# Attention's first chunk: gates read between the query taps, scores and turned keys moved forward into another pair of banks, and unread products in two holes

## What is computed

```python
k, v, q = (causal_dwconv(x @ W.T, cw, cb) for ...)        # four taps each
alpha, eta, theta = ...                                   # three rates per token, from x
for c0 in range(0, S, 128):                               # 8 chunks of 128 tokens
    g = grad of sum((silu(k W1') W2' - v)**2) in W1, W2   # at the chunk's first state
    g = 0.1 * g, clipped to norm 1
    per token: Sm = eta * Sm - theta * g;  Wm = (1 - alpha) * Wm + Sm
    h = silu(q . W1_t);  out_t = h . W2_t                 # with each token's own state
out = rmsnorm(out @ Wo.T) * norm_g * (x @ gW.T + gb)
x = x + out
```

## Time and profile before

| | |
|---|---|
| median of three runs | 743.92 us (741.38 to 745.2) |
| the profiled execution | 744.58 us |
| its span | 742.7 us |
| PE busy | 653.0 us, 88% |
| DVE busy | 567.4 us, 76% |
| ACT busy | 430.5 us, 58% |
| POOL busy | 247.9 us, 33% |
| attention, from its first to its last matmul | about 195 to 575 us of the span |
| mean granted TensorE clock | 0.958 of full |

### The profile page before, as it was taken

How to read it: one execution, slowest core, us unless ns; L and a number is a source line. 1 busy time by engine, 2 the same in 40 slices (tenths; PEclk the granted TensorE clock), 3 DMA queues, 4 the chain that set the end, 5 groups by cost and what they waited for, 6 DMA issues and landing times. The chain is left out here.

```text
span 742.7 us, 15297 instructions
## 1 busy us (share of the span) xinstructions
PE 653.0 (88%) x5555; PEld 573.8 (77%) x5555; DVE 567.4 (76%) x1379; ACT 430.5 (58%) x1094; POOL 247.9 (33%) x199
## 2 busy tenths in 40 slices
PE   4539999999697899999999999999988379999995
PEld 2238889898576788989888898988866158999985
DVE  0867888773388989898898988888676878887851
ACT  1416585562355767687786777776543445667450
POOL 0033453123311536162452516243241061751302
PEclk9759999999899999999999999999999589999998
DMA  9959727160332105325141432604123624652401
GB/s 337 413 207 349 268 96 263 48 209 23 128 115 86 59 29 162 97 82 177 57 136 66 132 126 59 200 2 139 62 66 105 227 75 164 237 193 113 142 8 36
DMA packets 63586, 101.98 MB, mean 137 GB/s; under 512 B 8200, under 2 KB 50336, under 8 KB 63392
## 3 DMA queue, kind: packets, MB, share of 16 engines
q1 hardware_dynamic: 51536, 83.01, 32.5%
q0 software_dynamic: 3840, 10.49, 4.3%
q10 hardware_dynamic: 8144, 7.61, 3.3%
HBM read 87.31 MB, written 22.16 MB: 147 GB/s over the span
## 5 line engine op out<-in xcount | busy, mean ns | idle before, releaser
L726 PE MATMUL ps<-moe_normedT_high,weights_high_up 128*128 128x320 f32 x252 | 80.5, 320 | 1.0 <-DVE moe_hidden_low L544 0.8
L727 PE MATMUL ps<-moe_normedT_low,weights_high_up 128*128 128x320 f32 x252 | 77.9, 309 | 0.0
L728 PE MATMUL ps<-moe_normedT_high,weights_low_up 128*128 128x320 f32 x252 | 77.9, 309 | 0.0
L726 PE MATMUL ps<-weights_high_down,moe_hidden_high 128*128 128x256 f32 x256 | 73.5, 287 | 0.0
L728 PE MATMUL ps<-weights_high_down,moe_hidden_low 128*128 128x256 f32 x256 | 71.7, 280 | 0.0
L727 PE MATMUL ps<-weights_low_down,moe_hidden_high 128*128 128x256 f32 x256 | 71.5, 279 | 0.0
L544 DVE SCALAR_TENSOR_TENSOR moe_hidden_low<-ps,moe_hidden_high 128x256 fp32r<-128x256 f32 x128 | 53.9, 421 | 22.7 <-ACT moe_hidden_high L681 18.6
L640 ACT CAST weights_high_down<-weights_raw_down 128x256 fp32r<-128x256 f32 x96 | 35.0, 406 | 39.1 <-PE ps L728 39.1
L1246 POOL TENSOR_TENSOR weights_raw_up<-weights_raw_up,att_AB 128x1024 f32<-128x1024 f32 x8 | 17.6, 2196 | 116.9 <-DVE att_ENDS L1454 116.9
L726 PEld LDWEIGHTS ps<-weights_high_down,moe_hidden_high 128*128 128x128 f32 x256 | 48.0, 188 | 3.1 <-issue 3.1
L318 DVE TENSOR_TENSOR weights_low_down<-weights_raw_down,weights_high_down 128x256 fp32r<-128x256 f32 x128 | 49.8, 416 | 0.0
(11 more groups left out here) (326 smaller groups left out, 2006.0 us busy)
## 6 DMA issues: line engine op xcount, KB each, us to landing
weights_raw_up<-in_w SPq DMA_DIRECT2D x16, 1024.0 KB, 8.7
weights_raw_down<-in_w SPq DMA_DIRECT2D x16, 1024.0 KB, 5.5
first_xt<-in_xT SPq DMA_DIRECT2D x8, 1024.0 KB, 8.1
weights_rows<-x SPq DMA_DIRECT2D x8, 1024.0 KB, 5.5
out_x<-weights_rows SPq DMA_DIRECT2D x8, 1024.0 KB, 4.5
weights_rows<-x ACTq DMA_DIRECT2D x7, 1024.0 KB, 5.5
att_AB<-decays_row SPq DMA_DIRECT2D x32, 129.0 KB, 2.9
att_eta<-rates_row SPq DMA_DIRECT2D x8, 512.0 KB, 4.1
```

Source lines behind the costliest of these rows:

```text
L726: mm(dst, high_l, high_r, start=start, stop=False)
L727: mm(dst, high_l, low_r, start=False, stop=False)
L728: return mm(dst, low_l, high_r, start=False, stop=stop)
```

## The change

It has these parts, all in chunk 0:

1. DVE reads gates 0 and 1 behind the first of the three query taps, gate 2 behind the last, gate 3 behind the small decay scans.
2. PE makes the scores ahead of the turned keys. The scores wait for two gate reads, where they waited for four; the turned keys go to `DD` and wait for three, where they went to `BB` and waited for four.
3. DVE makes `P1` right behind the scan `M` and ahead of `ends`; `KM` moves behind `dpre`, reads `DD` and waits for `k_squared` too.
4. ACT squares the turned keys ahead of the copy of the turned hidden layer, waiting for `k_turned` instead of `km_ready`.
5. PE makes four unread products, into a bank of `BB`, on each side of `residual`.

`scores` gets a wait for `m_ready` in all chunks; in the later ones the wait stands behind `ends`, which has it already.

```diff
-            def convolve_queries(c):
-                for n in range(1, TAPS):
+            def convolve_queries(c, taps=range(1, TAPS)):
+                for n in taps:
                     tap(c, (Q, raw_q, conv_q, q_conv), n)
+                if taps.stop < TAPS:
+                    return
...
                 if not first:
                     dve.wait_ge(state_made, c)
+                else:
+                    dve.wait_ge(k_squared, c + 1)
                 for n, own, _ in SIDES:
-                    last = v.tensor_tensor(KM[:, n, :, :], bc(wide(BB)[:, n, own].unsqueeze(2), [P, HALF, 2, D]),
+                    last = v.tensor_tensor(KM[:, n, :, :], bc(wide(DD if first else BB)[:, n, own].unsqueeze(2), [P, HALF, 2, D]),
...
             def scores(c):
                 dve.wait_ge(qk_made, c + 1)
+                dve.wait_ge(m_ready, c + 1)
...
             key_taps(0, 0, range(1, TAPS))
-            convolve_queries(0)
+            convolve_queries(0, range(1, 2))
+            gates(0, 0, (0, 1), True, True)
+            convolve_queries(0, range(2, TAPS))
+            gates(0, 0, (2,), True, True)
             decay_scans(0)
-            gates(0, 0, (0, 1), True, True)
+            gates(0, 0, (3,), True, True)
             momentum_scans(0)
-            gates(0, 0, (2, 3), True, True)
             memory_scans(0, True)
+            scores(0)
             ends(0, 0, True)
-            keys(0, 0, True)
-            scores(0)
             slope_of(0)
             residual(0)
+            keys(0, 0, True)
             key_norms(0, 0, first_k_sq)
...
             def keys(c, first, final=False):
-                if final:
+                if final or first:
                     act.wait_ge(k_turned, c + 1)
...
             normalise(1)
+            keys(0, True)
             hidden_turned(0, 0, True)
-            keys(0, True)
...
             def keys(c, par, first=False):
                 pe.wait_ge(kv_conv, TAPS * c + TAPS)
-                pe.wait_ge(gate_read, 4 * c + (4 if first else 3))
-                turn_keys(par, BB)
+                pe.wait_ge(gate_read, 4 * c + 3)
+                turn_keys(par, DD if first else BB)
 
-            def queries(c, par):
+            def queries(c, par, first=False):
                 pe.wait_ge(q_conv, TAPS * c + TAPS)
-                pe.wait_ge(gate_read, 4 * c + 4)
+                pe.wait_ge(gate_read, 4 * c + (2 if first else 4))
                 score(par, A)
...
             gate_pair(0, 3, FIRST_GATES[3])
+            queries(0, 0, True)
             keys(0, 0, True)
-            queries(0, 0)
             hidden_turned(0)
+            pe.wait_ge(gate_read, 4)
+            unread_products(4, 0, BB)
             residual(0, 0)
+            unread_products(4, 0, BB)
             step(0, 0, True)
```

More of the change, by code:

```diff
@@ L1786, in keys @@
                 for n, own, _ in SIDES:
-                    last = s.activation((first_k_sq if first else k_sq)[:, n, :], wide(BB)[:, n, own], ACT.Square)
+                    last = s.activation((first_k_sq if first else k_sq)[:, n, :], wide(DD if first else BB)[:, n, own], ACT.Square)
                 last.then_inc(k_squared, 1)
```

## The result

| | before | changed |
|---|---|---|
| median | 742.66 us (20 executions, 741.38 to 746.55) | 745.53 us (20 executions, 744.22 to 747.18) |
| ratio | | 1.0029, 95% interval 1.0018 to 1.0041 |
| profiled execution | 744.58 us | 744.22 us |
| its mean granted clock | 0.958 | 0.956 |

The change made the kernel slower, by 0.29% (2.2 us by the ratio; the medians differ by 2.9). The forecast was 743.9 us, no change. The measured 745.53 lies inside the forecast range and within the 0.5% called "same", but its interval is clear of no change. And yet the two profiled executions differ by 0.4 us, in favour of the changed kernel. The three runs of before that were at hand had their median at 743.92; over 20 it is 742.66. So the first thing to read is what the profile of the changed kernel shows, the second how far the profile of before stood for its kernel.

The account below looks back on a forecast made before the run. The prologue was taken as bound by a chain through PE to the projections; earlier work and the lost half clock at the keys were offset by the slope's delay and a new fall, giving 743.9 us, range 740.8 to 745.7.

Parts of the forecast that it names:

- Gates, scores, keys: Chunk 0 prologue: reordered gate reads and earlier scores start `turn_x` at 230.8 us, 4.1 us ahead; keys take 1.1 us.
- The slope's meeting with `hid_m`: Chunk 0 prologue: POOL's sum delays DVE's second slope pass, taken as 1.7 us, leaving the split 0.55 us ahead.
- The new hole and its fall: PE before chunk 0's projections: idle 5.1 us instead of 1.55, then half clock for some 3 us.
- The sum, for the profiled execution: Projection behind the queries' starts at 244.95 to 245.1 us, 0.0 to 0.2 later: no change against 744.58 us.
- the price of the new fall: Half clock at chunk 0's projections costs 1.5 us, taken from the 3.1 us of low clock at the keys.
- rival 4: At the projections the clock comes back late: 6.8 us low after PE resumes, costing 3.3 us; 745.7 us, chance 0.10.
- 24 matmuls in a row: Argument against a late return of the clock: PE has 24 matmuls in a row at the projections.
- The rate: Projections: a 512-column matmul takes 0.47 us at half clock, 0.24 at full, losing 0.48 us per low microsecond.
- the credit for the old fall: Chunk 0's keys and scores: their half clock, 3.55 us against about 2.2 at chunk 1, is gone.
- The base: Whole kernel: the forecast counts from the median of 743.92 us, 0.7 below the profiled 744.58; three runs spread over 3.8.
- The chances: Whole kernel: same within 0.5% (3.7 us) 0.85, faster by more 0.11, slower by as much 0.04.

Follow-up runs that it names:

- e5: The changed kernel as it is, timed and profiled again beside the kernel before: 745.44 us, ratio 1.0034.
- e15: The kernel before, unchanged, in one more profiled execution, which shows no fall of the clock at the keys: 742.03 us.
- e8: The changed kernel with `KM` put back between the ends and the slope: 744.02 us, ratio 1.0013 to the kernel before.

## Why the prediction was wrong

- *Gates, scores, keys*: right. `turn_x` at 230.8, it was 230.73; keys 1.1, it was 1.09. The gap before the residual was 0.33 us.
- *The slope's meeting with `hid_m`*: right. Second pass at about 2.4, it took 2.28; the split ahead by 0.55 us, it was 0.5 ahead counted from `att_zeros` (41.3 against 41.8).
- *The new hole and its fall*: right. 5.1 us, it was 4.88, with a fall in every profile.
- *The sum, for the profiled execution*: right. The projection behind the queries' was to start 0.0 to 0.2 us later; counted from `att_zeros` it started 0.15 earlier, at 49.50 against 49.65, and the two profiled executions differ by 0.4 us. This agreement hid the error, as it holds against an execution of before that had fallen.
- *The failed step, first part*: the price of the new fall. "I take 1.5, the price of the nearer hole" fits the executions with about 3 us of low clock behind the resumption, which cost 1.1 and 1.5 us against the filled hole. In two of four profiles the low stretch was 6.8 us, 4.7 and 6.1 of it behind the resumption, and cost 2.1 and 2.6. The four average 1.8. These two are rival 4, whose 745.7 us is near the measured 745.5, but it was given 0.10 and argued away by "24 matmuls in a row"; in e5 the clock stayed low through 6.1 us of them. The rate, 0.48 us lost per low microsecond, held roughly.
- *The failed step, second part*: the credit for the old fall. "The sum is no change, against the profiled execution of 744.58 us; it is 0.7 above the median of 743.92, and I count from the median." The sum set the new fall against the one at the keys as if every execution of before had that. e15 shows one that has not: there is nothing to be won back, and the changed kernel's ruler is 1.2 to 2.7 us longer than e15's. In how many executions the kernel before falls is open, so the share of this part in the 2.9 us is too. The 4.8 us for which the clock held from 187.97 to 192.8 could have been read as a sign that 2.4 us need not bring a fall.
- *The base*: the median of three, 743.92, was 1.3 us above that of 20. The forecast counted from it, so that much of its level was the luck of three executions. The medians of 20 differ by 2.9 us, of which the two parts explain up to 1.9; the rest stays open.
- *The chances*: "same" holds by its 0.5%. That the median fell into the range is owed to its upper end, which came from a rival given a tenth.

## What to carry to other kernels

A fall of the clock behind a short hole can be an event of one execution: before it is set off as a saving, take a second and third profile of the kernel before. A mean clock alone does not say where the clock fell. Making the work ahead of a join earlier, when the join itself hardly moves, gathers the holes into one. Here PE idled 6.0 us in four holes before and 5.4 in three after, 4.9 of it in one piece, and the rulers are 66.5 on average against 64.6 to 66.2; fill the longest hole, or do not open it. And when a DVE pass with two SBUF inputs moves, look what POOL runs at its new place.

## What the runs showed of the hardware that was not expected

Behind the same 4.9 us hole the low clock lasted 3.4 us in some executions and 6.8 in others of the same program. A hole of 2.4 us brought a fall in three of the four profiles of before on the faster chips and none in the fourth. A DVE pass over only 128x8 elements took 2.15 us beside a POOL instruction, and 0.17 in the next chunk (at 290.16). The two passes of `KM`, with one input in PSUM, kept their 1.29 us beside POOL (e8). Seventeen matmuls that nobody reads made the kernel 3.6 us faster.
